# The fp8 feed-forward block of layer 2: keeping the first pass's positive parts in SBUF

## The reference

```
def _fp8_matmul(x2d, w):
    scale_x = jnp.maximum(jnp.max(jnp.abs(x2d)) / FP8_MAX, 1e-06)      # FP8_MAX = 448
    scale_w = jnp.maximum(jnp.max(jnp.abs(w)) / FP8_MAX, 1e-06)
    x8 = (x2d / scale_x).astype(jnp.float8_e4m3fn)
    w8 = (w / scale_w).astype(jnp.float8_e4m3fn)
    out = jnp.matmul(x8.astype(x2d.dtype), w8.astype(x2d.dtype).T)
    return out * (scale_x * scale_w)
...
h = _fp8_matmul(x2d, w_fc)             # 2048 tokens x 2048 hidden units
h = jnp.square(jax.nn.relu(h))
out = _fp8_matmul(h, w_proj)           # 2048 tokens x 512
```

## Time and profile before

| | |
|---|---|
| median of 3 runs | 3404.22 us (3401.59 to 3406.93) |
| profiled execution, its own time | 3412.33 us |
| its span in the profile | 3410.3 us |
| mean granted TensorE clock | 0.901 of full speed |
| the stage `fp8_ffn` in the span | about 2814 to 3023 us |
| first pass, first matmul to last reduction | 2814.4 to 2875.9 us |
| second pass, first Relu to last add into x | 2879.2 to 3022.3 us |

### The profile page before, as it was taken

One profiled execution on the slowest core, in us unless ns is written; L12 is line 12 of the kernel. 1 busy time (PEld: TensorE's weight loads), 2 busy tenths in 40 slices (PEclk: granted clock), 3 DMA queues, 4 the chain that ended last, 5 costly groups with the idle time before them and its releaser, 6 DMA issues. The chain is left out here.

```text
span 3410.3 us, 63176 instructions
## 1 busy us (share of the span) xinstructions
PE 2727.4 (80%) x21404; PEld 1416.1 (42%) x21404; DVE 2490.0 (73%) x4757; ACT 1909.4 (56%) x2773; POOL 602.4 (18%) x539
## 2 busy tenths in 40 slices
PE   5768999686799999999996677686789628859983
PEld 3344444333465656565663433333211213334542
DVE  5746677656799999999994666624499796676548
ACT  2554433232599999999992533321578332844541
POOL 4341000012110101010104233303021610020013
PEclk8978999897899999999998888887899859978996
DMA  4433420200000000000000200010332010032301
GB/s 149 170 140 115 155 75 37 90 0 16 19 13 7 13 7 13 7 13 7 7 0 16 87 0 0 18 59 13 75 75 50 22 50 0 1 85 50 67 8 53
DMA packets 65341, 152.00 MB, mean 45 GB/s; under 512 B 11841, under 2 KB 20049, under 8 KB 63377
## 3 DMA queue, kind: packets, MB, share of 16 engines
q1 hardware_dynamic: 62368, 140.43, 13.8%
q0 software_dynamic: 2800, 9.18, 0.8%
HBM read 93.61 MB, written 24.38 MB: 35 GB/s over the span
## 5 line engine op out<-in xcount | busy, mean ns | idle before, releaser
L1617 DVE TENSOR_REDUCE s_top<-ps 128x1 f32<-128x512 f32 x1024 | 657.3, 684 | 30.4 <-PE ps L1512 29.9
L1586 ACT ACTIVATE s_prob<-ps,s_shift,m_sq 128x1024 int16<-128x1024 f32 x512 | 615.1, 1202 | 30.6 <-DVE s_shift L1625 30.6
L1512 PE MATMUL ps<-s_ks,s_qs 128*128 128x512 f16 x1024 | 352.5, 386 | 61.0 <-issue 14.8
L1517 PEld LDWEIGHTS ps<-ident,s_prob 128*128 128x128 f16 x4096 | 272.7, 98 | 123.5 <-DVE m_o L1635 51.5
L1517 PE MATMUL ps<-ident,s_prob 128*128 128x128 f16 x4096 | 314.2, 220 | 0.7 <-ACT s_prob L1586 0.5
L1505 PE MATMUL ps<-s_ks,s_qs 128*128 128x512 f16 x1024 | 307.5, 382 | 1.0 <-ACT s_prob L1586 0.5
L1592 ACT ACTIVATE s_probT<-ps 128x1024 f16<-128x1024 int16 x256 | 262.2, 1024 | 7.0 <-PE ps L1517 6.6
L1008 PE MATMUL ps<-m_hT,m_w 128*128 128x512 f16 x1024 | 232.3, 381 | 1.8 <-PEq L105 1.8
L249 PE MATMUL ps<-ident,s_parts 128*128 128x128 f16 x640 | 77.4, 296 | 129.2 <-POOL s_parts L240 127.5
L1630 DVE CAST s_probT<-ps 128x1024 f16<-128x1024 int16 x256 | 174.4, 681 | 4.7 <-PE ps L1517 4.7
L2289 DVE TENSOR_SCALAR s_prob<-ps,s_cap 128x1024 f32<-128x1024 f32 x128 | 158.2, 1270 | 25.8 <-PE ps L2198 25.8
(11 more groups left out here) (403 smaller groups left out, 5708.5 us busy)
## 6 DMA issues: line engine op xcount, KB each, us to landing
s_qs<-m_qT SPq DMA_DIRECT2D x144, 128.0 KB
s_ks<-m_kT SPq DMA_DIRECT2D x96, 128.0 KB
numbers<-s_numbers SPq DMA_DIRECT2D x21, 512.0 KB, 2.7
s_slabs<-numbers SPq DMA_DIRECT2D x21, 512.0 KB, 5.9
m_ks<-context_parts SPq DMA_DIRECT2D x12, 512.0 KB
expert_rows<-s_y SPq DMA_DIRECT2D x19, 256.0 KB, 2.0
s_rows_in<-in_ctx SPq DMA_DIRECT2D x16, 256.0 KB
x_sb<-in_L_ffn_W_up SPq DMA_DIRECT2D x4, 1024.0 KB, 6.0
```

Of the source, the lines that this page charges most:

```text
L1512: pe.matmul(quarter_at(q), qs[:, hb, bass.ds(t * P, P)], ks[:, hb, cols(q, 512)], start=True, stop=True).then_inc(s.top_scored, 1)
L1517: j = pe.transpose(turned(half, F16)[:, cols(m, P)], prob[:, u, cols(8 * half + m, P)].bitcast(F16), k.ident[:])
L1586: act.activation(prob[:, u, cols(half, HALF)], pair(half).rearrange("p m n -> p (m n)"), ACT.Exp, bias=shift[:, u:u + 1], scale=sq[:, bass ...
L1617: dve.tensor_reduce(top4[:, u, q:q + 1], quarter_at(q), AX.X, ALU.max).then_inc(s.top_read, 1)
```

## The change

In the first pass ScalarE now writes the positive part of each piece to SBUF, behind VectorE's reduction of the same bank. 62 pieces go to a new buffer `store` (128 x 62 x 512 fp32); the last two go into the memory of `wfc`, so their Relus wait until all reductions are done, by when TensorE has read `wfc` for the last time. The loop over the groups is written out, and TensorE waits for the Relu of the piece eight back, at every piece alike.

The second pass has no product with `wfc` and no Relu. ScalarE squares the kept piece in place, and VectorE makes `high` first and then `low`, from the kept piece. `low`, `high`, `above` and `hid` lie in the memory of `xT`, which the second pass no longer reads. TensorE only multiplies `hid` with `wproj`. The result banks alternate: even groups in banks 0 to 3, odd ones in 4 to 7, so TensorE waits for adds only of the group before the last. The whole second pass is one stream over 64 pieces; the adds of group g are put into VectorE's stream behind `hid` of the second piece of the next group, and those of the last group stand at the end. The load of ScalarE's function table stands behind the last Relu.

The diff, cut to its core:

```diff
+    PIECES = G * FC
+    EDGE = 128.0
+    LATE = 2
...
-        A, Q, LAG, YB = 4, 4, 4, 4
+        A, Q, LAG = 4, 4, 2
...
+        store = s.sb("store", [P, PIECES - LATE, GT], F32)
+        late = wfc.rearrange("p c f -> p (c f)")[:, 0:2 * LATE * GT].bitcast(F32)
+        spare = xT.rearrange("p c n -> p (c n)")
+        above = spare[:, 0:A * GT].rearrange("p (a n) -> p a n", a=A)
+        hid = spare[:, A * GT:(A + Q) * GT].rearrange("p (a n) -> p a n", a=Q)
+        low = spare[:, 4096:5120].bitcast(F8).rearrange("p (a n) -> p a n", a=A)
+        high = spare[:, 5120:6144].bitcast(F8).rearrange("p (a n) -> p a n", a=A)
+
+        def kept(i):
+
+            return store[:, i, :] if i < PIECES - LATE else late[:, cols(i - PIECES + LATE, GT)]
+
+        def y_bank(g, t):
+
+            return k.ps[:, 4 * (g % 2) + t, :]
...
         def _(pe):
+            for i in range(PIECES):
+                g, n = i // FC, i % FC
+                if i >= 8:
+                    pe.wait_ge(s.relu_ready, i - 7)
                 for c in range(DC):
+                    j = pe.matmul(k.ps[:, i % 8, :], wfc[:, c, cols(n, P)], xT[:, c, cols(g, GT)],
                                   start=(c == 0), stop=(c == DC - 1))
+                j.then_inc(s.first_ready, 1)
+            pe.wait_ge(s.relu_ready, PIECES)
             pe.wait_ge(s.spread, 1)
             pe.matmul(k.ps[:, 7, 0:P], wide_top[:], k.ident32[:], start=True, stop=True).then_inc(s.total_ready, 1)
+            pe.wait_ge(s.scale_ready, 1)
+            for i in range(PIECES):
+                g, n = i // FC, i % FC
+                if n == 0 and g >= 2:
+                    pe.wait_ge(s.y_used, TG * (g - 1))
+                pe.wait_ge(s.hid_ready, i + 1)
+                for t in range(TG):
+                    j = pe.matmul(y_bank(g, t), hid[:, i % Q, cols(t, P)], wproj[:, n, :],
+                                  start=(n == 0), stop=(n == FC - 1))
+                j.then_inc(s.hid_used, 1)
...
         def _(act):
+            for i in range(PIECES):
+                act.wait_ge(s.first_used, i + 1 if i < PIECES - LATE else PIECES)
+                act.activation(kept(i), k.ps[:, i % 8, :], ACT.Relu).then_inc(s.relu_ready, 1)
             act.preload_act_table(ACT.Square)
+            act.wait_ge(s.relu_ready, PIECES)
             act.wait_ge(s.root_ready, 1)
+
+            def above_edge(i):
+                act.wait_ge(s.high_ready, i + 1)
+                if i >= A:
+                    act.wait_ge(s.hid_ready, i - A + 1)
+                act.activation(above[:, i % A, :], high[:, i % A, :], ACT.Identity, bias=minus_edge[:, 0:1],
+                               scale=2.0).then_inc(s.above_ready, 1)
+
+            for i in range(PIECES):
+                act.activation(kept(i), kept(i), ACT.Square, scale=root[:, 0:1]).then_inc(s.square_ready, 1)
+                if i:
+                    above_edge(i - 1)
+            above_edge(PIECES - 1)
...
+            for i in range(PIECES):
+                dve.wait_ge(s.first_ready, i + 1)
+                dve.tensor_reduce(tops[:, i:i + 1], k.ps[:, i % 8, :], AX.X, ALU.max).then_inc(s.first_used, 1)
+            dve.wait_ge(s.first_used, PIECES)
...
+            def split(i):
+                dve.wait_ge(s.square_ready, i + 1)
+                if i >= A:
+                    dve.wait_ge(s.above_ready, i - A + 1)
+                dve.tensor_scalar(high[:, i % A, :], kept(i), EDGE, 0.5, ALU.max, ALU.mult, saturate=False
+                                  ).then_inc(s.high_ready, 1)
+                if i >= A:
+                    dve.wait_ge(s.hid_ready, i - A + 1)
+                dve.tensor_scalar(low[:, i % A, :], kept(i), EDGE, None, ALU.min, saturate=False
+                                  ).then_inc(s.low_ready, 1)
+
+            def finish(i):
+                if i >= Q:
+                    dve.wait_ge(s.hid_used, i - Q + 1)
+                dve.wait_ge(s.low_ready, i + 1)
+                dve.wait_ge(s.above_ready, i + 1)
+                dve.tensor_tensor(hid[:, i % Q, :], low[:, i % A, :], above[:, i % A, :], ALU.add).then_inc(s.hid_ready, 1)
+
+            def add(g):
                 dve.wait_ge(s.hid_used, FC * (g + 1))
                 for t in range(TG):
                     x = k.x[:, TG * g + t, :]
+                    dve.scalar_tensor_tensor(x, y_bank(g, t), factor[:, 0:1], x, ALU.mult, ALU.add).then_inc(s.y_used, 1)
+
+            for i in range(PIECES + LAG):
+                if i < PIECES:
+                    split(i)
+                if i >= LAG:
+                    finish(i - LAG)
+                if i >= FC + LAG + 1 and (i - LAG - 1) % FC == 0:
+                    add((i - LAG - 1) // FC - 1)
+            add(G - 1)
```

More of the change, by code:

```diff
@@ L2513, in fp8_ffn @@
 def fp8_ffn(k, xT, wfc, wproj, sx, sfc, sproj, gate):
-    with stage(k, "vsteps", "first_ready", "first_used", "max_ready", "spread", "total_ready", "scale_ready", "root_ready",
-               "power_ready", "a_ready", "relu_ready", "square_ready", "low_ready", "high_ready", "above_ready", "hid_ready",
+    PIECES = G * FC
+    EDGE = 128.0
+    LATE = 2
+    with stage(k, "vsteps", "first_ready", "first_used", "relu_ready", "max_ready", "spread", "total_ready", "scale_ready",
+               "root_ready", "power_ready", "square_ready", "low_ready", "high_ready", "above_ready", "hid_ready",
                "hid_used", "y_used") as s:
-        A, Q, LAG, YB = 4, 4, 4, 4
-        EDGE = 128.0
-        tops = s.sb("tops", [P, G * FC], F32)
+        A, Q, LAG = 4, 4, 2
+        tops = s.sb("tops", [P, PIECES], F32)
         top = s.sb("top", [P, 1], F32)
@@ L2530, in fp8_ffn @@
         factor = s.sb("factor", [P, 1], F32)
[L2531 to L2535, removed]
-        minus_edge = s.sb("minus_edge", [P, 1], F32)
-        hid = s.sb("hid", [P, Q, GT], F16)
+        minus_edge = s.sb("minus_edge", [P, 1], F32)
+        store = s.sb("store", [P, PIECES - LATE, GT], F32)
+        late = wfc.rearrange("p c f -> p (c f)")[:, 0:2 * LATE * GT].bitcast(F32)
@@ L2635, in _ @@
             v.done(dve.tensor_tensor(factor[:], factor[:], sh[:], ALU.mult))
[L2636 to L2661, removed]
@@ L2664, in _ @@
                     x = k.x[:, TG * g + t, :]
-                    dve.scalar_tensor_tensor(x, k.ps[:, YB + t, :], factor[:, 0:1], x, ALU.mult,
-                                             ALU.add).then_inc(s.y_used, 1)
+                    dve.scalar_tensor_tensor(x, y_bank(g, t), factor[:, 0:1], x, ALU.mult, ALU.add).then_inc(s.y_used, 1)
[7 more added lines that the diff above has]
+            add(G - 1)
 def attention_causal(k, qT, ks, ctx, keys_loaded, ctx_loaded, gate):
```

3 lines of the change are left out of this document (removed).

## The result

The changed kernel takes 3353.14 us (median of four runs, 3351.38 to 3359.28) against 3405.35 us (four runs, 3401.59 to 3406.93): a ratio of 0.9854, 95% interval 0.9842 to 0.9866. The forecast was 3353.8 us. The profiled execution took 3352.55 us with a span of 3350.5.

A forecast was written before the change was run, and what follows sets the result against it. ScalarE was taken to set the second pass's pace, passing to VectorE at 1.28 us a piece. Savings 47.4 + 3.4 - 0.4 = 50.4 us off the median 3404.22 gave 3353.8 us, own range 3347 to 3360.

The forecast's parts named there:

- The bound before: Second pass of the old kernel: ScalarE sets the pace inside a group, 1.93 us per piece.
- The first pass: First pass: 3.4 us saved, with the 64 Relus moved there hidden at price 0.
- the drain: First pass: the loop's wait empties the eight banks at three turns, costing 1.14 us each; removing it saves 3.4 us.
- rival 5: First pass: Relu, reduction and matmuls shut each other out of PSUM, 81 us more, 3435 us; chance 0.02.
- The hand-over: Between the passes: the last two Relus wait for the last reduction, 0.4 us lost.
- The second pass: Second pass: VectorE sets 1.28 us a piece, 95.7 us against 143.1, 47.4 us saved.
- the ramp: Start of the second pass: ScalarE leads up to the `high` of piece 3, at 3.85 us.
- rival 2: Second pass: VectorE no longer overlaps instructions or slows beside ScalarE, period 1.54 us, 15.6 us given back, 3369.4; chance 0.12.
- The tail: End of the second pass: 2.57 us of last VectorE operations, then 1.66 to the add and 2.73 for four.
- The adds and the clock: Second pass: three sets of adds cost 2.7 us each without waiting; TensorE's slow clock after idling costs 0.
- rival 1: Second pass: TensorE's slow matmuls after four restarts are charged, 1.6 us each, 6.4 us, 3360.2 us; chance 0.10.
- Rival 3: Second pass: TensorE at half clock throughout, 113.8 us instead of 95.7, 3371.9 us; chance 0.03.

The follow-up runs named there:

- experiment 1: Changed kernel with TensorE again waiting, at each group's first piece of the first pass, until VectorE reduced the group before: first pass 61.8 us, second 95.2.
- Experiments 4 and 5: Two runs on the changed kernel: VectorE's `low` left out, second pass 89.4 us; `low` put before `high` again, second pass 95.5 us.
- experiment 3: Changed kernel with two `hid` buffers instead of four: second pass 96.5 us, 1.3 more.
- experiment 2: Changed kernel with one set of result banks and the adds at each group's end: second pass 98.8 us, 3.7 more.
- experiment 7: Changed kernel repeated, 3352.42 us, beside a version making `hid` as the larger of `low` and twice a half written by ScalarE, 3334.25 us.

## Why the prediction was right

*The bound before.* That ScalarE set the pace was read from one line of waits and one piece. It fits: with Relu gone and TensorE's half of the work too, the period fell by 0.65 us, from ScalarE's 1.93 to VectorE's 1.28. No run took away the Relus alone, so that it was not TensorE's 1.73 rests on the waits: ScalarE waited for TensorE six times, three at the turns of the groups and three behind the slow clock, and in no other piece.

*The first pass.* Forecast 3.4 us saved, measured 3.22, with 0.5 us of scatter between runs; experiment 1 shows that it is the drain. The missing 0.2 is at the start: the third reduction comes 1.32 us after the second, 1.00 before, since TensorE's weight loads kept the half clock's spacing of 0.43 us some 0.5 us longer; the first comes 0.13 us sooner. The Relus cost nothing beside the reductions, as the row of attention had promised: behind the first three the reductions lie 0.86 us apart, and rival 5, which put its 81 us there, falls.

*The hand-over.* Forecast 0.4 us lost, measured 0.41. The rows of it:

```profile
2863.30 0.69 DVE L2610 TENSOR_REDUCE s_tops<-ps 128x1 f32<-128x512 f32 x1 [0.17 <-PE ps L2555]
2864.02 1.08 ACT L2576 ACTIVATE m_wfc<-ps 128x512 f32<-128x512 f32 x2 [1.13 <-DVE s_tops L2610]
...
2865.13 1.28 ACT L2577 ACT_TABLE_LOAD   x1
...
2865.16 0.49 PE L2560 MATMUL ps<-ident,s_wide_top 128*128 128x128 f32 x2 [1.90 <-ACT m_wfc L2576]
...
2867.70 1.33 ACT L2589 ACTIVATE s_store<-s_store,s_root 128x512 f32<-128x512 f32 x2 [1.29 <-POOL s_root L2603]
```

The two late Relus start 0.03 us after the last reduction and take 1.08 us together, the small matmul follows at once. It starts 1.17 us after the reduction's end where 1.24 was forecast, and the chain from it to the first Square takes 2.54 us instead of 2.45; the two misses cancel, and that is luck. The table load (L2577) is over at 2866.41 and the root at 2867.60; the first Square starts 0.10 us behind the root, against 0.04 us for the Relu in the kernel before. The extra drain of 1.38 us that the Trainium skill gives (ScalarE: Activation LUTs, section "What ACT_TABLE_LOAD costs") would end at 2867.79, later than the Square began; so it is not on the path in full here, and whether the 0.06 us is its remainder no run tells.

*The second pass.* Forecast 95.7 us, measured 95.2. Of the 0.5, the period gives 0.4 (60 pieces at 1.273 instead of 1.28) and the adds 0.2 (2.64 instead of 2.7, three times), and the ramp takes 0.1 back. The term that carried it, 1.28 us as the sum of three start distances and not of three durations (1.54), is what stands between this and rival 2, which would have been 15.6 us off. Experiments 4 and 5 show that it is VectorE's order and nothing around it. The tail is as copied from before:

```profile
2956.59 1.89 DVE L2642 TENSOR_TENSOR m_xT<-m_xT 128x512 f16<-128x512 fp8e4 x3
...
2960.14 2.73 DVE L2648 SCALAR_TENSOR_TENSOR x_sb<-ps,s_factor,x_sb 128x512 f32<-128x512 f32 x4 [1.66 <-PE ps L2568]
```

0.60 between the last `hid`s, 1.66 to the adds, 2.73 for four, as in the earlier trace rows.

*The adds and the clock.* The first set of adds, and what happens around it (L2648 adds, L2630 `high`, L2585 Identity, L2568 TensorE):

```profile
2893.27 2.71 DVE L2648 SCALAR_TENSOR_TENSOR x_sb<-ps,s_factor,x_sb 128x512 f32<-128x512 f32 x4
...
2895.91 0.41 DVE L2630 TENSOR_SCALAR m_xT<-s_store 128x512 fp8e4<-128x512 f32 x1
...
2896.36 0.72 ACT L2585 ACTIVATE m_xT<-m_xT,s_minus_edge 128x512 f16<-128x512 fp8e4 x1 [2.57 <-DVE m_xT L2630]
...
2897.32 1.04 PE L2568 MATMUL ps<-m_wproj,m_xT 128*128 128x512 f16 x4 [2.87 <-DVE m_xT L2642]
```

VectorE goes from `hid` into the adds and out into `high` without idling; ScalarE waits 2.57 us for it and TensorE 2.87. Then TensorE's clock (windows, columns as in the earlier trace rows):

```profile
2898.00:2900.00 2.00, 1.76 (x6) 0.51 (x5) 2.00 (x5) 2.00 (x4) 0.00 (x0) 0.70 0.00 0
2900.00:2902.00 2.00, 2.00 (x6) 0.76 (x5) 2.00 (x6) 2.00 (x4) 0.00 (x0) 0.50 0.00 0
2902.00:2904.00 2.00, 2.00 (x10) 0.80 (x9) 2.00 (x6) 2.00 (x5) 0.00 (x0) 0.94 0.03 8
...
2920.00:2926.00 6.00, 5.68 (x14) 2.03 (x15) 6.00 (x16) 6.00 (x11) 0.00 (x0) 0.50 0.00 0
```

It falls to half (0.50) a moment after TensorE has resumed and is back by 2904: some 3.4 us at the lower level, by the means of the windows. Behind the second adds it is lower from 2920 to 2926, about twice as long, and behind the third about 3.4 us again. No VectorE operation waits for TensorE in any of them. So rival 1's cause came true and its price did not, and experiment 3 shows what keeps it away: the ring of four. Its estimate of 6.4 us was far too high for a ring of two as well, which paid 1.3. The kernel before, whose Relus did wait for the slow TensorE, paid about 2.0 (experiment 2). Rival 3 needed the slow clock to last; no slow stretch of the second pass took more than about 7 us.

*What was mis-sized.* No term of the sum by more than 0.6 us. Beside the sum, TensorE idles 6.2 us after the small matmul and not about 4: the prediction's 4 us are those from the first Square to the first `hid`. And it idles 2.9 us at each set of adds, not 3.3. Neither is on the path. In the experiments the 1.66 us of the last group was used for groups in the middle, which wait 1.13, and the cost of a shorter ring was put at three to five times what it is.

## What to carry to other kernels

Add up start-to-start distances of unhindered instructions, taken from places where the engine did not wait, and not their durations: on VectorE here that is 1.28 against 1.54 us a piece, and it decided the forecast. After the slowest engine has been relieved the next one can stand close by (0.05 us here), so look at both before you work on either; the further gain came from moving work so that the engine with the extra duty (the adds) has slack, and the other a ring to run ahead in. A ring does the same for a slow stretch of TensorE: with four buffers it cost nothing, with two 1.3 us. An idle GpSimd was not a free engine beside VectorE.

## What the runs showed of the hardware that had not been expected

- A `hid` on GpSimd took 2.48 us in the mean of 16, twice the 1.2 us that its subtractions of this size take, and `low` and `high` beside it up to 1.32 us instead of 0.42: both sides lost.
- TensorE's clock did not fall at a fixed place behind the 2.9 us of idling. Behind the first adds it fell after it, once the next matmuls were running (granted 1.00 until 2898, 0.50 from 2900 to 2902), and the matmuls right behind the gap still ran at full speed. Behind the second adds it had begun to fall before TensorE resumed at 2920.32 (0.82 from 2918 to 2920). In the repetition of the changed kernel (experiment 7) it did not fall behind the first adds at all (1.00 from 2880 to 2923).
- Copy with a fixed factor on ScalarE, fp32 to fp8, takes 0.61 us and 0.52 to the next operation; Identity with a bias from memory, fp8 to fp16, 0.72 and 0.61.
